# Attention on one Trainium2 core: for every eighth row tile VectorE takes the sum of exponentials, and the statistics spread over half-steps

## The reference

```python
def attn(x, Wq, Wk, Wv, bias_table, ln_gamma, ln_beta):      # x: 8 x 1024 x 512, 16 heads of 32
    attn = softmax(einsum('bhsd,bhtd->bhst', q, k) * scale)
    attn = attn + rel_bias[None]
    out = einsum('bhst,bhtd->bhsd', attn, v) ...
    return (out - mu) * rsqrt(var + LN_EPS) * ln_gamma + ln_beta
xn = layernorm(x)
s = attn(xn, ...)
g = silu(spiking_ffn(xn))          # relu^2 feed-forward, 5 steps of a spiking recurrence
return x + s * g
```

## Time and profile before

| | |
|---|---|
| time before, median of 3 runs | 3539.49 us (3537.76 to 3540.11) |
| the profiled execution | 3539.38 us, its span 3537.6 us |
| TensorE busy | 97% of the span |
| ScalarE busy | 74%, nine tenths or more in all but the first of the attention part's slices |
| VectorE busy | 71% |
| GpSimd busy | 49% |
| granted TensorE clock, mean | 0.996 |

### The profile page before, as it was taken

How to read it: one execution, slowest core, us unless ns; L and a number is a source line. 1 busy time by engine, 2 the same in 40 slices (tenths; PEclk the granted TensorE clock), 3 DMA queues, 4 the chain that set the end, 5 groups by cost and what they waited for, 6 DMA issues and landing times.

```text
span 3537.6 us, 55268 instructions
## 1 busy us (share of the span) xinstructions
PE 3424.5 (97%) x19964; PEld 1440.8 (41%) x19964; DVE 2496.7 (71%) x3948; ACT 2628.4 (74%) x3926; POOL 1718.1 (49%) x997
## 2 busy tenths in 40 slices
PE   7999999999999999999999999999999999999996
PEld 3444444444444444433433433433433433433431
DVE  5555555555555545777888888888888788888887
ACT  6433333333333335999999999999999999999997
POOL 0012222111111123799675675675675675676662
PEclk9999999999999999999999999999999999999999
DMA  5122322332222222221422322322322322322322
GB/s 186 57 80 80 104 79 87 101 98 94 79 79 80 80 82 75 87 74 51 141 85 80 100 86 80 101 85 80 100 86 80 101 85 81 100 85 81 100 63 81
DMA packets 238751, 312.35 MB, mean 88 GB/s; under 512 B 96624, under 2 KB 132208, under 8 KB 238480
## 3 DMA queue, kind: packets, MB, share of 16 engines
q1 hardware_dynamic: 238480, 308.82, 28.1%
HBM read 174.65 MB, written 76.61 MB: 71 GB/s over the span
## 4 chain that ended last, share of the span: by engine, by line
ACT 37%; issue 10%; PE 8%; DVE 4%; SPq 1%; DMA 1%; ACTq 0%; DVEq 0%; POOL 0%; POOLq 0%
ACT recurrence_or_probs L1380 19%; ACT s_sb L1387 18%; DVE s_sb L1462 2%; PE misc L1249 2%; PE acc L1329 2%; PE s_ps L1309 2%; PE s_ps L1295 2%; DVE gate_or_tokens L1574 1%; DVE x_or_queries L1499 1%; SPq L253 0%; DMA xT<-xnT 0%; DVE outT L1482 0%; DVE gate_or_tokens L1577 0%; DMA x_or_queries<-sub_rows 0%; PE misc L1231 0%
## 5 line engine op out<-in xcount | busy, mean ns | idle before, releaser
L1462 DVE TENSOR_SCALAR_CACHE_REDUCE s_sb<-s_ps 128x1024 f32<-128x1024 f32 x998 | 1213.3, 1221 | 366.8 <-PE s_ps L1295 337.8
L1650 POOL TENSOR_TENSOR recurrence_or_probs<-recurrence_or_probs,toep 128x512 f32<-128x512 f32 (+1 forms) x375 | 1287.4, 3452 | 361.2 <-ACT recurrence_or_probs L1380 360.9
L1387 ACT ACTIVATE s_sb<-s_sb,nmax 128x1024 f32<-128x1024 f32 x998 | 1164.9, 1167 | 5.3 <-DVE s_sb L1462 5.3
L1380 ACT ACTIVATE recurrence_or_probs<-s_ps 128x1024 f32<-128x1024 f32 x1024 | 1059.3, 1036 | 6.5 <-PE s_ps L1309 6.4
L486 PE MATMUL ps_fc<-xnT_part,w_fc 128*128 128x512 f16 x3072 | 707.2, 380 | 4.5 <-DVE w_fc L734 4.5
L501 PE MATMUL ps_y<-w_pr,hid_part 128*128 128x512 f16 x3072 | 706.2, 380 | 3.5 <-issue 2.6
L127 POOL TENSOR_TENSOR recurrence_or_probs<-gate_or_tokens,beta_row 128x512 f32<-128x512 f32 x60 | 89.9, 1498 | 1110.0 <-DVE gate_or_tokens L182 1106.5
L658 ACT ACTIVATE relu<-ps_fc 128x512 f32<-128x512 f32 x256 | 152.8, 597 | 630.3 <-PE ps_fc L486 630.1
L842 DVE TENSOR_TENSOR hid<-relu 128x512 f32<-128x512 f32 x256 | 212.8, 831 | 510.4 <-ACT relu L658 510.4
L1329 PE MATMUL acc<-recurrence_or_probs,val 128*32 128x512 f32 x4096 | 545.1, 604 | 2.3 <-DVE recurrence_or_probs L1561 1.5
L486 PEld LDWEIGHTS ps_fc<-xnT_part,w_fc 128*128 128x128 f16 x3072 | 301.0, 98 | 368.9 <-issue 7.8
(11 more groups left out here) (172 smaller groups left out, 2673.1 us busy)
## 6 DMA issues: line engine op xcount, KB each, us to landing
toep<-table_rows SPq DMA_DIRECT2D x32, 2048.0 KB, 8.2
x_or_queries<-x_or_queries SPq DMA_DIRECT2D x384, 64.0 KB, 2.0
x_or_queries<-in_x SPq DMA_DIRECT2D x16, 1024.0 KB, 10.4
xnT<-xnT_part SPq DMA_DIRECT2D x32, 512.0 KB, 8.3
x_or_gate<-in_x SPq DMA_DIRECT2D x16, 1024.0 KB, 9.2
base<-x_or_gate SPq DMA_DIRECT2D x16, 1024.0 KB, 6.8
xT<-xnT SPq DMA_DIRECT2D x32, 512.0 KB, 9.6
result<-gate_or_tokens SPq DMA_DIRECT2D x64, 256.0 KB, 2.0
```

What stands on the lines that cost most here:

```text
L1380: nc.scalar.activation(prob[:, k % PROBS, 2 * second:2 * second + 2, :].rearrange("p j n -> p (j n)"), s_ps[:, item_buffer(pair_item(m)), ...
L1387: nc.scalar.activation(s_sb[:, i % 4, :], s_sb[:, i % 4, :], ACT.Exp, bias=nmax[:, par, j, st:st + 1], scale=-1.0, accum_out=den[:, par, j ...
L1462: nc.vector.tensor_scalar(s_sb[:, i % 4, :], s_ps[:, item_buffer(tile_item(n)), :], -1.0, None, ALU.mult, ALU.min, accum_out=nmax[:, par, ...
L1650: nc.gpsimd.tensor_tensor(tile, tile, toep[:, par, :, at:at + width], ALU.add).then_inc(biased, 1)
```

## The change

Tiles whose number is 26 or more and a multiple of eight (124 of them) are exponentiated without a sum. VectorE reduces the exponentiated copy with an addition three half-steps later (`add_up`), behind the minimum of that half-step: in h = 1, 9, 17 and 25. The logarithm on ScalarE also waits for these sums, and the minimum that reuses the place of such a tile waits for its reduction. The statistics move from h = 0, 1, 2, 3 to h = 0, 3, 5, 7, and `root` from the end of half-step 9 to the end of half-step 13.

```diff
-STATISTICS = {0: 0, 1: 1, 2: 2, 3: 3}
+STATISTICS = {0: 0, 3: 1, 5: 2, 7: 3}
+ADDED, ADDED_LAG = 8, 3
+            def tile_earlier(self, h):
+                n = self.g * 32 + h + AHEAD - ADDED_LAG
+                return (n // 32, n // 32 % 2, n % 32) if AHEAD <= n < NG * 32 and summed_by_vector(n) else None
+        def summed_by_vector(n):
+            return n >= AHEAD and n % ADDED == 0
+        def added_up_to(n):
+            return (n + ADDED - 1) // ADDED - (AHEAD + ADDED - 1) // ADDED
             def exp_sum(G, par, i):
-                nc.scalar.activation(s_sb[:, i % 4, :], s_sb[:, i % 4, :], ACT.Exp, bias=nmax[:, par, j, st:st + 1], scale=-1.0,
-                                     accum_out=den[:, par, j, st:st + 1]).then_inc(sum_done, 1)
+                if summed_by_vector(n):
+                    nc.scalar.activation(s_sb[:, i % 4, :], s_sb[:, i % 4, :], ACT.Exp, bias=nmax[:, par, j, st:st + 1],
+                                         scale=-1.0).then_inc(sum_done, 1)
+                else:
+                    nc.scalar.activation(s_sb[:, i % 4, :], s_sb[:, i % 4, :], ACT.Exp, bias=nmax[:, par, j, st:st + 1], scale=-1.0,
+                                         accum_out=den[:, par, j, st:st + 1]).then_inc(sum_done, 1)
             def ln_sums(G, par, half):
                 act.wait_ge(sum_done, G * 32 + half * 16 + 16)
+                wait(act, added, added_up_to(G * 32 + half * 16 + 16))
-                    if k == 4 and s.finish and s.step == 0:
+                    if k == 6 and s.finish and s.step == 0:
                         root(s.done)
             def row_max(G, par, i):
                 dve.wait_ge(s_done, n + 1)
                 wait(dve, sum_done, n - 3)
+                if summed_by_vector(n - 4):
+                    dve.wait_ge(added, added_up_to(n - 3))
+            def add_up(G, par, i):
+                n = G * 32 + i
+                j, st = i % 16 // 4, i // 16 * 4 + i % 4
+                dve.wait_ge(sum_done, n + 1)
+                nc.vector.tensor_reduce(den[:, par, j, st:st + 1], s_sb[:, i % 4, :], AX, ALU.add).then_inc(added, 1)
                     if tiles:
                         row_max(tiles[0], tiles[1], tiles[2] + second)
+                    if s.tile_earlier(h):
+                        add_up(*s.tile_earlier(h))
                     take_misc(b, hg, s, h)
```

More of the change, by code:

```diff
@@ L991, in attention @@
         pv_done = sem("pv_done")
+        added = sem("added")
         biased = sem("biased")
```

## The result

The changed kernel takes 3592.7 us (median of 4 runs, 3591.4 to 3593.5) where the kernel before takes 3539.8: a ratio of 1.0149, 95% interval 1.0132 to 1.0167. It is 53 us slower; the forecast was 3 us faster.

The account below looks back on a forecast made before the run. ScalarE was taken to bound the kernel. Even slots -0.4, odd slots -2.2, five slots without the stretch -1.8 and the last +1.1 gave -3.3 us against 3539.4: 3536.1, predicted as 3536.0, range 3528 to 3543.

Parts of the forecast that it names:

- What bounds the kernel: Attention: ScalarE sets the pace at 2.04 us a half-step; waits for VectorE's minima total 5.3 us in 2000 us.
- the full stretch of VectorE: Half-steps 18 to 24 of a finishing slot, where VectorE was said to work without a gap.
- What leaves ScalarE: 124 sums lose their readout, 0.09 us a tile, 11.2 us in all; the sum within the exponential is free.
- What comes to VectorE: 124 reductions of 128x1024 after the minima of half-steps 1, 9, 17 and 25, at 1.25 us each.
- its signal: The minimum behind a reduction waits for the reduction's signal, put at 0.03 to 0.04 us.
- The stretch from 17: Finishing slots from half-step 17: net -0.03 us an even slot (-0.4 in all), -0.17 an odd one (-2.2).
- Moving `root`: From half-step 9 to 13: TensorE and minimum 17 come 0.14 us earlier in even slots.
- The statistics: Spread over half-steps 0, 3, 5 and 7: no gain by itself, room for the reduction of half-step 1, hidden.
- the margin 0.76: VectorE's margin at half-step 8, the tightest place in the new order of the statistics, in us.
- if that cover were short by x, it would cost x in 14 slots: Should VectorE's margin at half-step 8 not hide the moved statistics, each of 14 slots loses the shortfall.
- Rival (b): Slower: GpSimd's bias adds hold up the reductions at half-steps 1, 9, 17 and 25; +17.7 us, 3554; chance 0.10.
- The last slot: VectorE has no gap from minimum 1 to minimum 5, so the reduction adds its pitch: +1.1 us.

Follow-up runs that it names:

- e9: e5 with the second normalised tile at half-step 24 instead of 21: 3534.2 us.
- e10: As e9, but six reductions a slot, at half-steps 1, 9, 12, 15, 25 and 29: 3533.1 us.
- the one-port kernel: The changed kernel, with the addition of epsilon also writing out a minimum that nobody reads: 3544.7 us.
- e2: The kernel before with only the statistics and root moved, no reductions: 3587.3 us.
- e4: The kernel before with the fourth statistic at half-step 5 and root behind 13, no reductions: 3552.7 us.
- e7: The changed kernel, with GpSimd's bias add of key step 3 on 256 instead of 512 columns: 3546.9 us.
- e8: The kernel before with the second normalised tile at half-step 24 instead of 21: 3533.6 us.
- e5: The one-port kernel without the reductions at half-step 17 and of tile 1016, 92 reductions left: 3533.7 us.
- e11: As e9, with the reductions of half-steps 1 and 9 alone (60 of them): 3528.6 us.
- e6: As e5, with the two normalised tiles at half-steps 17 and 20 instead of 19 and 21: 3607.0 us.

## Why the prediction was wrong

**What bounds the kernel**: right for ScalarE, and the full stretch of VectorE is where I had it. That TensorE stands within 0.1 us of it from 12 to 28 was named only as a thing to watch at half-step 28. It showed where something else held TensorE up: in the changed kernel the half clock at half-step 11, in e9 and e10 the wait for VectorE ahead of pair 28.

**What leaves ScalarE**: right. A sum without readout has a pitch of 1.04 (ScalarE's timeline in the changed kernel):

```profile
2786.79 1.14 ACT L1403 ACTIVATE s_sb<-s_sb,nmax 128x1024 f32<-128x1024 f32 x1
2787.83 1.01 ACT L1395 ACTIVATE recurrence_or_probs<-s_ps 128x1024 f32<-128x1024 f32 x1
```

**What comes to VectorE**: the reduction right (1214 ns), its signal wrong. I took 0.03 us for the minimum that waits for it, from another engine's wait; it is 0.15, so the pitch of a reduction with a waiter is 1.37, not 1.25 (VectorE's timeline, the changed kernel):

```profile
2758.41 1.22 DVE L1491 TENSOR_REDUCE den<-s_sb 128x1 f32<-128x1024 f32 x1
2759.78 1.22 DVE L1484 TENSOR_SCALAR_CACHE_REDUCE s_sb<-s_ps 128x1024 f32<-128x1024 f32 x1 [0.15 <-DVE den L1491]
```

**The stretch from 17**: right but for that. ScalarE's new wait before sum 23 in odd slots is 0.22 us in the one-port kernel, as forecast. In that kernel, which has all of the change but the hold-up, an undisturbed even slot takes 66.76 us against 66.67 before: +0.09, where I had -0.03 and the 0.12 more of the signal makes +0.09. Odd slots -0.04, I had -0.17, again 0.12. Moving `root` was put at 0.14: the one-port kernel's even slots are 0.13 shorter than those with the statistics back (66.76, 66.89). The statistics moved along with it, so `root` alone wasn't measured.

**The statistics**: this is the step that failed. "The fourth with its aggregation takes 2750.36 to 2752.29 = 1.93", and I carried this 1.93 to half-step 7, as if it were work. Of it 0.88 was one instruction on four columns, which alone takes 0.17; the other 0.71 was a wait that the trace shows as busy. It depended on what GpSimd did at half-step 3, and at 7 GpSimd does something else: the price became 4.26, the margin 0.76 became -2.6, the wait before sum 8 is 2.8, and an even slot is 4.1 us longer (13 x 4.1 = 53; slot 30 adds 3.1, and the rest of the program is 4 us shorter). Against the one-port kernel the 4.0 us of slot 20 are 2.8 before sum 8, 0.8 at half-steps 11 and 12 and 0.4 before sum 20. The last two are what e2's slots without a fall of the clock don't have. My "if that cover were short by x, it would cost x in 14 slots" had the wait about right (x = 2.6), but the forecast has nothing of the 1.2 that came with TensorE's half clock. Rival (b) had the mechanism, GpSimd's adds holding VectorE up by SBUF, and I weighed it for the added instruction alone. The Trainium skill (SBUF — State Buffer, Who interferes with whom), which I cited for the reduction, says in the same place that scalar operations between SBUF tensors can run in a mode that takes the port pair shared with GpSimd, that the form which also writes its accumulator doesn't, and that the first to start holds the pair for its whole instruction. The traces agree: 4.26 against 0.16 us for the two forms beside the same add; the plain form ended 0.02 to 0.03 us after the add in all 14 even slots from 4 on, in each of six kernels (the kernel before, the changed one, e2, e4, e7, e8); and the reductions took 1206 to 1217 ns. In all these rows GpSimd was first; they don't show what happens when VectorE is.

**The last slot**: I had +1.1 us; it is as long as before (the pitches of sums 1 to 2 and 3 to 4 are 2.49 and 2.61 us where 2.05 and 3.04 stood). The normalised tiles that GpSimd holds up there lasted at most 1.67 us instead of 2.10.

**Not in the forecast at all**: the load of `xT`. In every second even slot from 6 on TensorE's first projection waits for it: six waits, 4.7 us, in the one-port kernel, none before. Why the load lands too late there wasn't tested. The one-port kernel's profiled execution took 3541.5 us, 5.4 above my sum: even slots +5.7 (these waits above all), odd slots +1.7, the last slot -1.1, and -0.9 in what comes before and the slots without the stretch. Its median is 3544.7, and what makes that 3 us longer no profile shows. So even without the hold-up the change was 5 us slower than the kernel before, outside my range: the signal (26 x 0.12 = 3.1 us) and the load (4.7) together cost more than the 3.3 us that I had as the gain. From the list of TensorE's waits in the one-port kernel, 1500 to 3500 us:

```profile
PE misc L1265 <- DMA xT<-xnT: 4.7, 6, 2.1
```

## What to carry to other kernels

An instruction whose duration doesn't fit its size (0.88 us for four columns) is waiting, though the trace calls it busy: find what the other engines do at its end before it is moved, and price it from the place where it goes. A long standstill of TensorE can cost twice, once as the wait and again through its granted clock: in e2 2.6 us of standstill, then in most slots 0.6 to 1.3 us more at half clock. And when engines are close to each other, a saving counts only in a slot where no other engine's chain ends later: three saved readouts gave 0.28 us an odd slot with the tile at 21 (e5) and nothing with it at 24 (e9), where VectorE kept TensorE waiting; without the reduction at 25 the two that were left arrived (e11).

## What the runs showed of the hardware

A VectorE scalar operation of 128x4 float32 from SBUF to SBUF takes 0.17 us alone and 0.88, 2.09, 2.24 or 4.26 beside a GpSimd tensor operation, each time until that one ends; with an accumulator written too it takes 0.16 and 0.08 for the readout, beside the same GpSimd operation. A two-input operation of 128x512 takes 0.75 alone and 3.72 beside it. A one-input reduction (1206 to 1217 ns) and the batch-norm statistics (676 to 694) aren't touched. TensorE's granted clock fell to 0.50 behind a standstill of 2.5 us in 14 of 14 slots of the changed kernel, of 2.6 in eleven of 14 of e2, of 2.4 in four of nine and of 1.8 in five of 13 of e6, and of 1.1 in none of e4's; at 0.50 eight products took 1.94 us instead of 1.06. A VectorE instruction that waits for the signal of the one directly ahead, a 1024-element reduction, starts 0.15 us after its end. ScalarE's accumulator readout costs a pitch of 0.09 us, and the sum within the exponential nothing.
